# Last block of a two-layer adaLN transformer with experts: expert outputs go back to their tokens by fp32 matmuls with a gated slot-by-token matrix, instead of by indirect picks

## The reference, cut to what matters

```python
capacity = int(T / E * CAP_FACTOR)                 # 1024 / 8 * 1.25 = 160
probs = softmax(x @ Wr)                            # 8 experts
topk_probs, topk_experts = top_k(probs, 2)
onehot  = one_hot(e_flat, E)
pos_all = cumsum(onehot, axis=1) - onehot          # place of a token in its expert's queue
keep = pos < capacity                              # later ones are dropped
buf[e, b, pos] += x * keep
h = relu(einsum('ebnc,ech->ebnh', buf, W1) + b1)   # 128 -> 512
y = einsum('ebnh,ehc->ebnc', h, W2) + b2           # 512 -> 128
y_tok = y[e_flat, b_idx, pos_c] * keep * p_flat
out = y_tok.reshape(B, T, K, C).sum(axis=2)        # two experts' rows summed per token
# the block then gives x + gb * out
```

## Time and profile before

| | |
|---|---|
| median of three runs | 1499.44 us |
| profiled execution, first to last instruction | 1502.4 us |
| PE busy | 1240.4 us (83%) |
| PE weight loads | 775.4 us (52%) |
| DVE busy | 981.4 us (65%) |
| ACT busy | 913.6 us (61%) |
| POOL busy | 526.9 us (35%) |
| `tail` | from 1163.4 us to the end, 339 us |

### The profile page before, as it was taken

The page is one execution under the profiler, slowest core; times in us unless marked ns, Lnnn a source line. Parts: engine busy times, 40 slices in busy tenths (PEclk is TensorE's granted clock), DMA queues, the critical chain, the costliest instruction groups (busy, mean ns, idle before and its releaser), DMA issues. The chain is left out here.

```text
span 1502.4 us, 26537 instructions
## 1 busy us (share of the span) xinstructions
PE 1240.4 (83%) x8185; PEld 775.4 (52%) x8186; DVE 981.4 (65%) x2622; ACT 913.6 (61%) x1319; POOL 526.9 (35%) x588
## 2 busy tenths in 40 slices
PE   6996768978987589999999999999998995656560
PEld 4875668978854223333433343333334874455550
DVE  5563466666668498888888888878887674421222
ACT  4562623323365588888888888878886664233320
POOL 6245745466286411221112111211120024444444
PEclk9998879999978899999999999999999897687885
DMA  9700022322245532222222122212200501102222
GB/s 271 226 1 28 25 64 84 103 71 82 77 151 187 120 46 35 38 34 36 36 37 36 39 37 38 40 42 38 40 8 9 168 17 48 51 31 67 77 60 73
DMA packets 114775, 100.33 MB, mean 67 GB/s; under 512 B 10882, under 2 KB 99424, under 8 KB 114656
## 3 DMA queue, kind: packets, MB, share of 16 engines
q1 hardware_dynamic: 101256, 78.64, 21.6%
q0 software_dynamic: 8192, 16.79, 3.9%
q10 hardware_dynamic: 5208, 3.43, 1.0%
HBM read 54.51 MB, written 44.30 MB: 66 GB/s over the span
## 5 line engine op out<-in xcount | busy, mean ns | idle before, releaser
L2426 ACT ACTIVATE probs<-scores_ps 128x1024 f32<-128x1024 f32 x512 | 507.1, 1027 | 81.3 <-PE scores_ps L2453 76.5
L2453 PE MATMUL scores_ps<-q_pack,k_pack 64*128 64x512 f32 x1024 | 245.2, 491 | 38.6 <-ACT probs L2426 21.2
L2470 PE MATMUL pv_ps<-probs,v_pad 128*32 128x512 f32 x2048 | 274.4, 608 | 0.2 <-DVE pv L2587 0.2
L2453 PEld LDWEIGHTS scores_ps<-q_pack,k_pack 64*128 64x128 f32 x1024 | 96.0, 184 | 310.6 <-issue 164.7
L2346 POOL TENSOR_TENSOR squares<-sparse_scores 128x512 f32<-128x512 f32 x32 | 41.0, 1281 | 471.3 <-DVE sparse_scores L2591 471.3
L1386 ACT ACTIVATE hidden_experts<-pre_experts 128x512 f32<-128x512 f32 x94 | 59.3, 631 | 130.6 <-DVE pre_experts L1320 66.1
L2663 DVE TENSOR_SCALAR_CACHE_REDUCE junk<-sparse_scores,at 128x1024 f32<-128x1024 f32 x96 | 122.8, 1279 | 3.4
L1408 PE MATMUL up_ps_experts<-x_t_experts,up_weights_now_experts 128*128 128x128 f32 x752 | 107.7, 288 | 17.9 <-DVE up_weights_now_experts L1315 10.9
L1408 PEld LDWEIGHTS up_ps_experts<-x_t_experts,up_weights_now_experts 128*128 128x128 f32 x752 | 95.3, 199 | 23.5 <-DVE up_weights_now_experts L1315 17.2
L3225 POOL DMA_INDIRECT expert_rows_dram<-expert_input_tail,send_to_tail x64 | 61.5, 962 | 127.6 <-DVE send_to_tail L3367 109.3
L1415 PE MATMUL down_ps_experts<-weights_t,hidden_experts 128*128 x736 | 98.8, 278 | 0.0
(11 more groups left out here) (406 smaller groups left out, 2412.1 us busy)
## 6 DMA issues: line engine op xcount, KB each, us to landing
q_pack<-q_pieces_dram SPq DMA_DIRECT2D x120, 64.0 KB
k_pack<-k_pieces_dram SPq DMA_DIRECT2D x120, 64.0 KB
expert_rows_dram<-zeros SPq DMA_DIRECT2D x1, 6400.0 KB, 22.2
x_rows_experts<-expert_rows_dram SPq DMA_DIRECT2D x25, 256.0 KB
expert_rows_dram<-y_rows_experts SPq DMA_DIRECT2D x46, 128.0 KB
q_pieces_dram<-q_pieces_prep SPq DMA_DIRECT2D x8, 512.0 KB, 3.6
k_pieces_dram<-k_pieces_prep SPq DMA_DIRECT2D x8, 512.0 KB
expert_rows_dram<-zeros SPq DMA_DIRECT2D x1, 2560.0 KB, 17.7
```

The lines of the kernel that those rows point to most:

```text
L2426: act.activation(probs[:, kt % 2, 2 * pair : 2 * pair + 2, c * 512 : c * 512 + 512], scores_ps[n % 2][:].rearrange("p (h t) -> p h t", h=2 ...
L2453: ins = pe.matmul(scores_ps[n % 2][:, head * 512 : head * 512 + 512], k_pack[group % 2][rows, pair, kt * P : kt * P + P].bitcast(F32R), q_ ...
L2470: ins = pe.matmul(pv_ps[32 * j : 32 * j + 32, c, :], v_pad[:, group % 2, kt, j, :], probs[:, kt % 2, j, c * 512 : c * 512 + 512], start=(k ...
```

## The change

1. Rows in the DRAM table grow from 128 to 132 numbers (`ROW1`): the token's number, the rank of its best expert, the gate of its second expert, and the difference of the two gates (`AT_TOKEN`, `AT_BEST`, `AT_SECOND_GATE`, `AT_MORE`). They are sent and loaded with the row.
2. `gates` runs per batch, before the send, and with it `exps` (Exp on ACT), where both ran once for all batches before.
3. `store_y`, `pick` and `combine` go. In their place DVE finds each slot's gate (`sg`, three small operations a batch) and builds, for each of the 10 tiles of slots, a 128 x 1024 matrix whose entry is the slot's gate where the column is the slot's token, and 0 elsewhere (`gt`, `place_tile`). PE multiplies each with the tile of expert outputs and sums over all slots in PSUM (`mix`: 5 parts a batch, each 2 tiles of slots x 8 tiles of tokens = 16 fp32 matmuls of 128x128x128), and DVE adds the two halves to x (`add`). `out_ps`, free once the dense part is over, holds the sums; four matrices go round (`PLACES`).
4. `turn_y` and `keep_y` go by 2 tiles rather than 4, all on ACT, and start as soon as the experts that they need are done, not after the last one.
5. A send is one transfer per entry of the list (`send.b.i`), and `TAIL_ORDER` is another list throughout.
6. POOL makes the constant tables first (`tables`); the clearing of the DRAM table is done in pieces of 66 numbers.

```diff
+AT_TOKEN, AT_BEST, AT_SECOND_GATE, AT_MORE = C, C + 1, C + 2, C + 3
+ROW1 = C + 4
...
+        pieces = -(-self.width // C)
+        piece = self.width // pieces
+        eng.dma_start(
+            self.rows[0 : self.cleared].rearrange("(p n) (h c) -> p (n h) c", n=n, h=pieces), zeros[:, 0:piece].unsqueeze(1).to_broadcast([P, n * pieces, piece])
+        ).then_inc(sem, 16)
...
 TAIL_ORDER = """
-turn_ctx.0 turn_ctx.1 keep_ctx.0 dense.0 keep_ctx.1 attended.0 turn_ctx.2 keep_ctx.2 root1.0 invert1.0 dense.1 turn_ctx.3 keep_ctx.3 cols norm1.0
...
+turn_ctx.0 cols keep_ctx.0 dense.0 colk turn_ctx.1 attended.0 turn_ctx.2 keep_ctx.1 keep_ctx.2 turn_ctx.3 dense.1 turn_ctx.4 root1.0 keep_ctx.3
...
                 def load_x(b):
                     sp.wait_ge(rows_sent[b], 16 * 2 * NT)
                     if b >= 2:
-                        sp.wait_ge(y_stored[b - 2], 16)
+                        sp.wait_ge(mix_made, mixed(b - 2, MIX_PARTS - 1, 1))
...
-                def store_y(b):
-                    for n in range(len(TURN_PARTS)):
-                        sp.wait_ge(turn_free[turns.at("y", b, n)], turns.emptied_with("y", b, n))
-                    sp.dma_start(rows(expert_rows.rows[b * SLOTS : (b + 1) * SLOTS, :]), expert_io[:, b % 2]).then_inc(y_stored[b], 16)
...
+                def send(b, i):
+                    k, n = i // NT, i % NT
+                    if i == 0:
+                        step.settle()
+                        pool.wait_ge(send_ready, b + 1)
+                        pool.wait_ge(gates_ready, b + 1)
+                        pool.wait_ge(n_ready[2], HT * (2 * b + 2))
+                    pool.indirect_dma_start(
+                        expert_rows.rows, bass.IndirectOffsetOnAxis(ap=send_to[:, b, k, n : n + 1], axis=0), n3[:, b % 3, n, :], None
+                    ).then_inc(rows_sent[b], 16)
...
+                def gates(b):
+                    row = n3[:, b % 3]
+                    dve.wait_ge(exps_ready, b + 1)
...
+                    step(dve.reduce_sum(total[:], exps[:, 0 : NT * E].rearrange("p (n e) -> p n e", e=E), AX.X))
+                    step(dve.tensor_copy(row[:, :, AT_BEST], rank[:, 0]))
+                    step.settle()
+                    step(dve.reciprocal(total[:], total[:]))
+                    step.settle()
+                    step(dve.tensor_tensor(row[:, :, AT_SECOND_GATE], exps[:, NT * E : NT * (E + 1)], total[:], ALU.mult))
+                    step.settle()
+                    dve.tensor_tensor(row[:, :, AT_MORE], total[:], row[:, :, AT_SECOND_GATE], ALU.subtract).then_inc(gates_ready, 1)
+
+                def slot_gates(b):
+                    gate, row = slot_gate[:, b % 2], expert_io[:, b % 2]
+                    dve.wait_ge(tables_made, TABLE_STEPS)
+                    dve.wait_ge(x_loaded[b], 16)
+                    step(dve.tensor_tensor(gate, row[:, :, AT_BEST], slot_rank[:], ALU.is_equal))
...
+                def place_tile(b, t):
+                    at = b * SLOT_TILES + t
+                    if at >= PLACES:
+                        dve.wait_ge(mix_made, 2 * ((at - PLACES) // MIX_TILES + 1))
+                    dve.tensor_scalar(
+                        place[:, at % PLACES, :], token_no[:], expert_io[:, b % 2, t, AT_TOKEN : AT_TOKEN + 1], slot_gate[:, b % 2, t : t + 1], ALU.is_equal, ALU.mult
+                    ).then_inc(placed, 1)
+
+                def add(b, h):
+                    x = g.x[:, half(2 * b + h), :]
+                    dve.wait_ge(mix_made, mixed(b, MIX_PARTS - 1, h))
+                    dve.tensor_tensor(flat(x), out_ps[h][:], flat(x), ALU.add).then_inc(combined, 1)
...
+                def exps_of(b):
+                    act.wait_ge(sel_ready, b + 1)
                     act.activation(exps[:], shifted[:], ACT.Exp).then_inc(exps_ready, 1)
...
+                def turn_y(b, p):
+                    last = ((p + 1) * MIX_TILES * P - 1) // CAPACITY
+                    pe.wait_ge(down_free, downs.number(b, last))
+                    turn(("y", b, p), MIX_TILES, lambda i: ye_t[:, (p * MIX_TILES + i) * P : (p * MIX_TILES + i) * P + P])
+
+                def mix(b, p):
+                    turned("y", b, p)
+                    pe.wait_ge(placed, b * SLOT_TILES + (p + 1) * MIX_TILES)
...
+                    for h in range(2):
+                        for t in range(p * MIX_TILES, (p + 1) * MIX_TILES):
+                            for i in range(HT):
+                                n = h * HT + i
+                                ins = pe.matmul(
+                                    out_ps[h][:, i * C : i * C + C],
+                                    place[:, (b * SLOT_TILES + t) % PLACES, n * P : n * P + P],
+                                    expert_io[:, b % 2, t, 0:C],
+                                    start=(t == 0 and i == 0),
+                                    stop=(t == SLOT_TILES - 1 and i == HT - 1),
+                                )
+                        ins.then_inc(mix_made, 1)
```

More of the change, by code:

```diff
@@ L3005 @@
-ff_relu.5.3 root3.4 y_res.5 ff_relu.5.2 best.1 keep_n1.6 ff_down.5 keep_y2.6 norm1.7 pos.1 invert3.4 index.1 ff_up.6.0 ff_up.6.1 ff_out.5 norm3.4
-turn_n1.7 ff_relu.6.0 ff_relu.6.1 turn_n3.4 ff_up.6.2 keep_n1.7 root2.5 ff_up.6.3 ff_relu.6.2 y_res.6 ff_relu.6.3 ff_up.7.0 ff_down.6 invert2.5
-keep_n3.4 logits.4 update.5 root3.5 load_x.0 invert3.5 norm3.5 ff_out.6 turn_n3.5 ff_relu.7.0 ff_up.7.1 turn_x.0.0 keep_n3.5 root2.6 keep_x.0.0
-logits.5 turn_x.0.1 ff_relu.7.1 ff_up.7.2 keep_y2.7 turn_x.0.2 keep_x.0.1 ff_relu.7.2 ff_up.7.3 keep_x.0.2 y_res.7 invert2.6 go_up.0.0.0 ff_relu.7.3
@@ new lines @@
+send.0.13 ff_relu.7.1 turn_n3.4 gate.1 ff_up.7.2 keep_n3.4 send.0.14 index.1 ff_up.7.3 root3.5 ff_relu.7.2 send.0.15 ff_relu.7.3 ff_out.6 logits.4
+send.1.0 load_x.0 y_res.7 ff_down.7 send.1.1 invert3.5 root2.6 send.1.2 invert2.6 norm3.5 update.6 send.1.3 turn_x.0.0 turn_x.0.1 keep_x.0.0 send.1.4
+keep_x.0.1 turn_x.0.2 send.1.5 sg.0 root3.6 turn_n3.5 keep_x.0.2 ff_out.7 keep_n3.5 send.1.6 go_up.0.0.0 go_up.0.0.1 relu.0.0.0 logits.5 send.1.7
+relu.0.0.1 go_up.0.1.0 best.2 go_up.0.1.1 root2.7 send.1.8 relu.0.1.0 go_down.0.0 relu.0.1.1 send.1.9 go_up.0.2.0 go_up.0.2.1 relu.0.2.0 gt.0.0
@@ new lines @@
+send.1.10 pos.2 exps.2 bias.0.0 go_up.0.3.0 gt.0.1 send.1.11 go_down.0.1 index.2 relu.0.2.1 send.1.12 relu.0.3.0 go_up.0.3.1 gate.2 relu.0.3.1
+go_up.0.4.0 send.1.13 bias.0.1 go_up.0.4.1 gt.0.2 turn_y.0.0 send.1.14 go_down.0.2 invert2.7 keep_y.0.0 gt.0.3 mix.0.0 send.1.15 relu.0.4.0 bias.0.2
+invert3.6 relu.0.4.1 send.2.0 load_x.1 update.7 norm3.6 send.2.1 go_up.0.5.0 turn_n3.6 send.2.2 go_up.0.5.1 keep_n3.6 gt.0.4 go_down.0.3 root3.7
+send.2.3 gt.0.5 logits.6 relu.0.5.0 sg.1 send.2.4 turn_x.1.0 bias.0.3 relu.0.5.1 go_up.0.6.0 invert3.7 turn_y.0.1 go_up.0.6.1 send.2.5 keep_y.0.1
@@ new lines @@
+go_up.1.1.0 gt.1.3 go_up.1.1.1 relu.1.1.0 pos.3 bias.1.0 relu.1.1.1 add.0.1 go_up.1.2.0 index.3 go_down.1.1 relu.1.2.0 store.1 go_up.1.2.1 sg.2
+send.3.0 go_up.1.3.0 bias.1.1 relu.1.2.1 turn_x.2.0 turn_y.1.0 relu.1.3.0 send.3.1 go_down.1.2 store.0 keep_y.1.0 go_up.1.3.1 send.3.2 bias.1.2
+go_up.1.4.0 relu.1.3.1 mix.1.0 send.3.3 relu.1.4.0 send.3.4 send.3.5 go_up.1.4.1 gt.1.4 go_down.1.3 relu.1.4.1 gt.1.5 send.3.6 go_up.1.5.0 bias.1.3
+go_up.1.5.1 relu.1.5.0 send.3.7 go_down.1.4 relu.1.5.1 send.3.8 go_up.1.6.0 bias.1.4 go_up.1.6.1 relu.1.6.0 go_down.1.5 send.3.9 relu.1.6.1
```

242 lines of the change are left out of this document (107 added, 135 removed).

## The result

The changed kernel took 1494.24 us in the median (1489.07 to 1498.31, 14 runs), the kernel before beside it 1502.01 (1498.35 to 1508.16, 14 runs). The ratio is 0.9946, with a 95% interval of 0.9931 to 0.9960: 0.5% faster, 8 us. The forecast was 1494.6. PE is busy 1299.4 us (1240.4 before), the span is 1494.5 (1502.4), its mean granted clock 0.939 of full speed (0.913).

The account below looks back on a forecast made before the run. PE bounds the tail, except in POOL's bursts of indirect transfers, which stall it. PE's end 1468.4 + 71.8 - 52.8 + 4.0 = 1491.4, plus 6.2 is 1497.6, -4.8 against span 1502.4; from the median 1494.6 us, range 1482 to 1510.

Parts of the forecast that it names:

- the store at the end: Behind PE's last matmul: store of the result after the last sum, 5.4 us of the 6.2 us end chain.
- PE's end: End of PE's work in the tail: 1468.4 before, forecast 1491.4 us.
- `mix`: Tail on PE: 20 parts, 320 fp32 matmuls at 3.59 us a part, +71.8 us with nothing to hide them.
- Bursts: POOL's 16-transfer bursts in the tail: 17.6 us each; three picks beside PE's work go, -52.8; four sends unchanged.
- Extras: Tail: six more table loads on ACT 2.5 us, hand-offs before `mix` 1.5 us; +4.0 in the sum.
- Four separate bursts: Sends in the tail: at least seven us of each interval worked off after the burst, so four bursts at 17.6 each.
- No waits beside the last `mix`: Sign in the last 100 us: no window with PE under 90%.
- 1 (`mix` inside the bursts): Faster: PE does one `mix` part in the stall of each of the last three sends, -11, 1484 us; chance 0.18.
- 2 (hand-offs): Slower: PE waits at 20 `mix` parts for ACT's copy and DVE's matrices, 18 for 1.5, 1511 us; chance 0.17.
- 3 (matrices hold up the sends): Slower: some 20 DVE matrices lengthen the last three bursts by up to 14 us; 1505 us, chance 0.10.
- 4 (sends fuse): Slower: gaps between sends shrink, two bursts lose their first 8 us of work, +16, 1511 us; chance 0.05.
- wrong altogether: If POOL's transfers don't cause the stall: sends alone wouldn't stall 17.6 us, or the last 100 us would without them.

Follow-up runs that it names:

- e12: Kernel before, each send and pick waiting until the one two before it has landed: 1472.38 us, ratio 0.9791, with stalls.
- e4: Kernel before, POOL's 64 indirect picks replaced by four plain DMAs a batch on SP: 1441.33 us, ratio 0.9593.
- e7: Kernel after, matmuls of one of the two slot tiles in each part of mix left out: 1361.74 us, ratio 0.9976, without stalls.
- e1: Kernel after, POOL's 64 indirect sends replaced by two plain DMAs a batch on SP, sorting left out: 1433.84 us, ratio 0.9557.
- e8: Kernel after, Copy in place of Exp for the gates, 7 table loads fewer: 1392.46 us, ratio 1.0198, without stalls.
- e3: Kernel after, each send waiting until the one before it has landed: 1488.57 us, ratio 0.9912.
- e6: Kernel after, a POOL memset behind each send that the next waits for, one send every 1.8 us: 1410.93 us, ratio 1.0336, without stalls.
- e5: Kernel after, at most two sends under way, by two semaphores a batch: 1399.77 us, ratio 1.0255, without stalls.
- e10: The kernel of e5 again (after, at most two sends under way), with stalls: 1469.60 us, ratio 0.9783.
- e11: The kernel of e6 again (after, one send every 1.8 us), with stalls: 1447.32 us, ratio 0.9627.

## Why the prediction was right, point by point

*The forecast.* 1494.6 against 1494.24. Much of that is luck. The forecast was a difference of -4.8 from a median of 1499.44; the difference was -8 from one of 1502.0. The step that missed it by 3 us is the store at the end. It was priced at 5.4, read from the start of the last sum's store to the span's end in before. In after the last sum ends at 1491.80 and the span at 1494.5: 2.7. I took for the store's own time a stretch that isn't the same behind another chain: it is 5.4 again in e12, which ends with POOL's picks, and 2.8 in e4, which doesn't.

*PE's end.* Forecast 1491.4, measured 1491.1. The sum held, its terms less well. With what the runs give for them, 1468.4 + 71.8 to 74.6 (`mix`) - 43 (picks), it comes to 1498 to 1500 even without the table loads, 6 to 9 us too late. That it held is luck in part: the price of 17.6 counted ordinary waits in with the stall, and waits that no run prices one by one left with the change too. The terms:
- `mix`: +71.8 forecast, 74.6 busy (276 ns a record), most or all of it in the time (e7). Forecast and row differ by 2.8 in the counting and not in the clock: nearly every part takes 3.73 us in the timeline, as `ff_down` takes 3.74 in that of before (1187.15), for which the chain of waits gave the 3.59 of the forecast.
- Bursts: 17.6 forecast, by elapsed time less work. By removal 15 (e1) for sends and 14.2 (e4) for picks. The difference to 17.6 is not the burst's: it is made of ordinary waits, which stay when the burst goes. The three picks beside PE's work were worth 43 us and not 52.8, and those waits left with the old order or came with the new; the runs don't separate that.
- Extras: the table loads stayed open (0 to 7.3, e8); eight of 1283 ns are there in the tail's table-load rows, four for Exp and four for the way back.
- Four separate bursts: right. They begin at 1238.0, 1276.7, 1312.3 and 1368.2, and in each the first 7 to 9 us are worked through. By elapsed time less work they cost 18.2 each, near the 17 to 18 named as a sign; by removal 15.
- No waits beside the last `mix`: PE is busy 20 of 20 us in every such stretch from 1410 on.

*The rivals.* 1 (`mix` inside the bursts): no. `mix.1.0` ran in burst 4, but in its first 7 us, which are free anyway; then PE waited like the rest. 2 (hand-offs): falls, 0.0 idle before `mix`. 3 (matrices hold up the sends): small, but hardly put to the test. Of some 20 matrices expected beside sends only four stood there, in part since DVE stops in a stall too; two of the four issues beside them took 1.09 and 1.22 us instead of 0.96, and a matrix took 810 ns in the mean instead of 679. The Trainium skill's rule, page "SBUF — State Buffer", section "SBUF: two separate sides", would have POOL stand still for each matrix. The trace of e8, where DVE works through the bursts, is nearer to it than that of after: an issue begun beside the first of two matrices took 1.76 us and ended 0.12 us behind the second, the rows below. 4 (sends fuse): no, though e3 and e6 show what it had at stake, since rows that come later are waited for.

```profile
1236.92 1.76 POOL L3260 DMA_INDIRECT expert_rows_dram<-expert_input_tail,send_to_tail  x1 [0.30 <-issue]
...
1237.76 0.80 DVE L3419 TENSOR_SCALAR gated_place_tail<-token_no_tail,expert_rows_now_tail,slot_gate_tail 128x1024 f32<-128x1024 f32 x1
```

*What the prediction didn't see.* It took the stall for a fixed price of a burst. It is the price at one level. Without stalls, before takes 1365 us: 138 less, and after 94 to 104 less (e5 and e8). If the front gains the same 37 us in both (the first send of e5 is at 1202.4, of e10 at 1239.9, and the front has 128 such transfers), 101 us remain for the seven bursts beside PE's work in before and 57 to 67 for the four in after: 14 to 17 each, by a third way that rests on this assumption. There the change loses 28 to 35 us: PE's 72 to 75 us of `mix` and the 4 of extras (the forecast's figure) buy an end chain shorter by some 31, if it is as long there, and rid it of three rounds of picks that, by subtraction, cost only 10 to 20 there. The forecast named this danger only as "wrong altogether, if the stall in a burst came from something other than POOL's transfers".

*What stays open.* Why the stall is there on one occasion and not on another; whether it is there at all when no execution is recorded, since most records of the transfers' ends are missing where it stands; what the engines then wait for ("remote"); and why two transfers under way stop them for half as long while a pace of 1.8 us doesn't stop them at all. A run of after at the level without stalls is missing.

## What to carry to other kernels

Price a stall by taking its cause away and not by elapsed time less work, which counts all ordinary waits in with it (17.6 against 15 us). Before buying fewer transfers with 75 us of matmuls, try to pace them: a 0.5 us memset between sends, in the changed kernel, gave 3.2 to 3.4% where there were stalls, the change itself 0.4 to 0.5%; without stalls the memset kernel is 11 us slower than e5. Time the kernel before again beside every group of experiments; a change whose whole gain is fewer stalls has the other sign where there are none. And where a trace calls a releaser "remote" or gives no time to landing, ask first whether its records are complete.

## What the runs showed of the hardware that was not expected

- With stalls, some 8 us after a row of POOL's indirect transfers begins (one per 1.26 us, 67.6 KB each), PE, DVE and ACT stop, and go on some 3 us after the last issue, at a DMA share of 0.16. At one per 1.78 us they work on through sixteen and more (e11).
- The same sends at the same pace let the engines work on at the other level (PE 11.37 of 12 us, e8). Over the whole kernel before, the levels differ by 138 us, 9%.
- Where there are stalls, three quarters of the records of the sends' ends are missing (62 of 256 in the first batch of after), where there are none hardly any (256 of 256 in e8). Sends one at a time leave all of them (e3). Whether the stall is one of the recording isn't shown.
- In the first stall of after PE, idle from 1247.3, has a granted clock of 0.50, that is 1.2 of 2.4 GHz, from 1254 on, and 1.00 again from 1270, some 9 us after it went back to work.
